# A transformer block with linear attention and routed experts: query chunks started inside the key stage, a reordered passage into the feed-forward stage, and GpSimd's bias sums gathered at the end of the key stage

## What is computed

```python
def attention(x, w_qkv, proj, w_out, b_out):          # x: (4, 1024, 128), 16 heads of 8
    q, k, v = split(x @ w_qkv)
    qp = elu1(einsum('bhnd,hdf->bhnf', q, proj))      # 32 features a head
    kp = elu1(einsum('bhnd,hdf->bhnf', k, proj))      # elu1(a) = a + 1 if a > 0 else exp(a)
    kv = einsum('bhnf,bhnd->bhfd', kp, v)
    den = einsum('bhnf,bhf->bhn', qp, kp.sum(2)) + 1e-8
    return (einsum('bhnf,bhfd->bhnd', qp, kv) / den) @ w_out + b_out

def ffn(x, wr, br, w1, b1, w2, b2):                   # 8 experts, 128 -> 512 -> 128
    e = argmax(x @ wr + br)
    return gelu(x @ w1[e] + b1[e]) @ w2[e] + b2[e]

x = layernorm(x + attention(x, ...))
out = layernorm(x + ffn(x, ...))
```

## Time and profile before

| What | Value |
|---|---|
| Time, median of 3 runs (lowest to highest) | 234.96 us (234.77 to 235.1) |
| The profiled execution's own time | 234.93 us |
| Its span, first to last instruction | 233.2 us |
| PE busy | 202.8 us (87%), 1727 matmuls |
| DVE busy | 154.7 us (66%) |
| ACT busy | 140.2 us (60%) |
| POOL busy | 133.4 us (57%) |
| Mean granted TensorE clock | 0.962 of full |
| Bytes moved | 40.45 MB, 173 GB/s on the mean |
| Chain that ended last, by engine | PE 55%, issue 13%, POOL 12%, DVE 8% |

### The profile page before, as it was taken

One profiled execution on the slowest core, in us unless ns is written; L12 is line 12 of the kernel. 1 busy time (PEld: TensorE's weight loads), 2 busy tenths in 40 slices (PEclk: granted clock), 3 DMA queues, 4 the chain that ended last, 5 costly groups with the idle time before them and its releaser, 6 DMA issues.

```text
span 233.2 us, 5949 instructions
## 1 busy us (share of the span) xinstructions
PE 202.8 (87%) x1727; PEld 159.0 (68%) x1734; DVE 154.7 (66%) x530; ACT 140.2 (60%) x366; POOL 133.4 (57%) x171
## 2 busy tenths in 40 slices
PE   7989999999799998898888389899899999999700
PEld 2668888888555554545442279798799999999600
DVE  1577686877476999889989233247557677777720
ACT  3488887878477576866564045455466667666400
POOL 8329284646500104776768617655776588888770
PEclk9999999999999999999999679999999999999955
DMA  4899999999760000111011467650477678874100
GB/s 119 217 379 409 414 408 410 411 414 375 220 178 0 0 6 12 35 35 47 27 35 46 147 175 217 195 138 20 154 221 220 201 229 236 233 182 133 35 6 0
DMA packets 28416, 40.45 MB, mean 173 GB/s; under 512 B 3497, under 2 KB 18126, under 8 KB 28384
## 3 DMA queue, kind: packets, MB, share of 16 engines
q1 hardware_dynamic: 26112, 35.80, 47.5%
q0 software_dynamic: 2272, 4.27, 5.3%
HBM read 17.95 MB, written 22.56 MB: 174 GB/s over the span
## 4 chain that ended last, share of the span: by engine, by line
PE 55%; issue 13%; POOL 12%; DVE 8%; DMA 4%; ACT 4%; SPq 1%; POOLq 1%; DVEq 0%; ACTq 0%
PE pair L753 15%; PE pair L299 12%; PE pair L768 10%; POOL sorted_rows L504 9%; PE bank L615 4%; PE bank L768 4%; PE pair L746 2%; DMA x_all<-sorted_rows 1%; DVE qexp L969 1%; PE pair L585 1%; POOL rstd L476 1%; ACT qexp L829 1%; DMA w_slot<-in_L_ffn_w_dram 1%; PE bank L595 1%; PE pair L765 1%
## 5 line engine op out<-in xcount | busy, mean ns | idle before, releaser
L912 ACT ACTIVATE qfeat<-pair,w_sb 128x128 f32<-128x128 f32 x156 | 44.7, 368 | 29.1 <-PE pair L753 28.5
L753 PE MATMUL pair<-xsT,w_slot 128*128 128x128 f32 x312 | 42.4, 280 | 1.7 <-DMA w_slot<-in_L_ffn_w_dram 1.2
L504 POOL DMA_INDIRECT sorted_rows<-x,dest x32 | 33.4, 1043 | 17.1 <-DVE dest L1115 9.9
L753 PEld LDWEIGHTS pair<-xsT,w_slot 128*128 128x128 f32 x312 | 38.7, 195 | 2.4 <-issue 2.4
L299 PE MATMUL pair<-wkv_part,xT_all 128*128 128x256 f32 x192 | 33.8, 320 | 2.0 <-ACT vals L839 0.8
L299 PEld LDWEIGHTS pair<-wkv_part,xT_all 128*128 128x128 f32 x192 | 28.3, 188 | 5.5 <-issue 5.5
L768 PE MATMUL pair<-w_sb,qfeat 128*128 x232 | 31.5, 279 | 0.0
L534 POOL TENSOR_TENSOR ksum<-kfeat 128x512 f32<-128x512 f32 x12 | 16.5, 1372 | 24.9 <-DVE kfeat L978 24.9
L525 POOL DMA_INDIRECT out_dram<-x_all x26 | 26.3, 1010 | 7.0 <-issue 5.7
L768 PEld LDWEIGHTS pair<-w_sb,qfeat 128*128 128x128 f32 x232 | 28.2, 192 | 0.9
L476 POOL TENSOR_TENSOR rstd<-var_eps,minus_half 128x4 f32<-128x4 f32 x8 | 8.3, 1041 | 31.4 <-DVE var_eps L1051 31.4
(11 more groups left out here) (181 smaller groups left out, 405.8 us busy)
## 6 DMA issues: line engine op xcount, KB each, us to landing
sorted_rows<-pad_rows SPq DMA_DIRECT2D x11, 1584.0 KB, 22.9
w_slot<-in_L_ffn_w_dram SPq DMA_DIRECT2D x39, 256.0 KB, 3.1
x_all<-in_L_attn_x_dram SPq DMA_DIRECT2D x8, 256.0 KB, 5.4
w_sb<-in_L_ffn_w_dram SPq DMA_DIRECT2D x4, 512.0 KB, 14.0
x_all<-sorted_rows SPq DMA_DIRECT2D x26, 66.0 KB, 2.6
xs<-sorted_rows SPq DMA_DIRECT2D x13, 66.0 KB, 2.3
w_sb<-in_L_ffn_b_dram SPq DMA_DIRECT2D x1, 512.0 KB, 7.2
sorted_rows<-x,dest POOLq DMA_INDIRECT x32, 2.5
```

Of the source, the lines that this page charges most:

```text
L504: g_.indirect_dma_start(out=sorted_rows, out_offset=bass.IndirectOffsetOnAxis(ap=dest[:, ring, i:i + 1], axis=0), in_=x1[:, ring, i, :], i ...
L753: last = mm(h_bank[t % 2][:, k * P:(k + 1) * P], w1_slot[:, t % WB, k * P:(k + 1) * P], xsT[:, t % 2, :], start=True, stop=True)
L912: a_.activation(hT[:, t % 2, k * P:(k + 1) * P], h_bank[t % 2][:, k * P:(k + 1) * P], ACT.Gelu, bias=w2_sb[:, bass.ds(w_at[t] + (FF + D + ...
```

## The change

**Key stage.** GpSimd keeps only the router score (`score_base`) in the loop; the eight sums of x and output bias run one after the other when the loop is over. Three of the four query chunks of group 0 move into the last steps on PE, with their exponentials on ACT and two of DVE's `q_features` ahead of `keep_kv(3)`; the banks of the chunks are rotated by one for that.

**Query stage.** DVE's group step has the same instructions in another order. ACT takes the third exponential ahead of the layer norm.

**Passage.** Both layer norms of GpSimd go to ACT: group 6's at once, group 7's a quarter at a time after the first four tile steps. On PE `project(7)` and `ranks(6)` go ahead of `turn(0)`, with four more unread matmuls between them, and `ranks(7)` comes two tile steps earlier. DVE makes the experts' part of the first table earlier (8 steps, `TAB_E`), and SP asks for the weights of tiles 0 to 3 then; from there on it asks for the weights two tiles ahead of the rows. DVE adds the bias of every tile, so the twenty one-row matmuls in the profile (two for each of tiles 0 to 9) go. The first four batches are normalised one step later.

```diff
-        TAB_A, TAB_B = 14, 16
+        TAB_E, TAB_A, TAB_B = 8, 14, 16
...
-        def offset(eng, kind, table, t, most):
+        def offset(eng, kind, table, t, most, first=TAB_A):
             if t == 0:
-                eng.wait_ge(tab_step, TAB_A)
+                eng.wait_ge(tab_step, first)
...
-        q_bank = [bank[0], bank[1], bank[2], bank[7]]
+        q_bank = [bank[7], bank[0], bank[1], bank[2]]
...
+            def load_weights(t):
                 reach(sp, hid_pre, t - WB + 1)
-                at = offset(sp, ENG.SP, e_tab, t, (E - 1) * FF)
+                at = offset(sp, ENG.SP, e_tab, t, (E - 1) * FF, TAB_E)
                 sp.dma_start(w1_slot[:, t % WB, :], w1_pieces[bass.ds(at, FF), :].rearrange("(p c) d -> p (c d)", c=FC)
                              ).then_inc(w1_loaded[t % WB], 16)
+            for t in range(4):
+                load_weights(t)
             for i in range(XR):
                 sp.wait_ge(scattered[i], 16 * GT * len(range(i, GA, XR)))
             for t in range(NA):
                 load_rows(t)
-
+                if 4 <= t + 2 < NA:
+                    load_weights(t + 2)
+
+            for t in (NA, NA + 1):
+                load_weights(t)
             for i in range(XR):
                 sp.wait_ge(scattered[i], 16 * GT * G // XR)
             sp.wait_ge(res_ready, G)
             for t in range(NA, NT):
                 load_rows(t)
+                if t + 2 < NT:
+                    load_weights(t + 2)
             sp.wait_ge(stored, 16 * NT)
...
+            def score_base(g):
+                tiles = slice(g * GT, (g + 1) * GT)
...
-            def layer_norm(g):
-                par, ring = g % 2, g % XR
-                pool.wait_ge(shift_ready, g + 1)
-                pool.wait_ge(rstd_ready, g + 1)
-                for i in range(GT):
-                    last = g_.tensor_scalar(x1[:, ring, i, 0:D], res[:, par, i, :], rstd[:, par, i:i + 1], shift[:, par, i:i + 1],
-                                            ALU.mult, ALU.add)
-                last.then_inc(x1_ready, 1)
...
-                    residual_base(u // 2)
+                    score_base(u // 2)
+            pool.wait_ge(const_in, 16 * 2)
+            for g in range(G):
+                residual_base(g)
             for s in range(G):
                 group_step(s)
             scatter(G - 4, range(GT))
             token_numbers(G - 2)
             inverse_deviation(G - 2)
-            layer_norm(G - 2)
             scatter(G - 3, range(0, 2))
             token_numbers(G - 1)
             inverse_deviation(G - 1)
             scatter(G - 3, range(2, GT))
-            layer_norm(G - 1)
             scatter(G - 2, range(GT))
...
+            def q_chunk(g, k):
+                n = g * C + k
+                reach(pe, q_done, n - QB + 1)
+                if n in (1, 2):
+                    pe.wait_ge(k_done, T - 1)
+                    pe.wait_ge(v_ready, T - 1)
+                mm(q_bank[n % QB][:, :], ones_bf[:, :], share[:, :].to_broadcast([P, 512]), start=True, stop=False)
+                product(q_bank[n % QB], wq_part[:, :, k * P:(k + 1) * P], xT_all[:, :, g * 512:(g + 1) * 512],
+                        [(slice(0, 512), slice(0, 512))], start=False).then_inc(q_pre, 1)
+
             turn_group(0)
...
             for u in range(UT + 3):
+                if u == UT + 2:
+                    q_chunk(0, 2)
...
                 if 0 <= u - 1 < UT:
+                    if u == UT:
+                        q_chunk(0, 0)
                     add_kv(2 * u - 2)
                     if (u - 1) % UB:
                         add_pair_sum(u - 2)
+                    if u == UT:
+                        q_chunk(0, 1)
                     add_kv(2 * u - 1)
...
-                if t not in BIASED_BY_DVE:
-                    mm(y_bank[t % 4][:, 0:D], ones_row[:, :], w2_sb[0:1, bass.ds(w_at[t] + FF, D)], start=True, stop=False)
                 for k in range(FC):
                     pe.wait_ge(hT_ready, FC * t + k + 1)
                     last = mm(y_bank[t % 4][:, 0:D], hT[:, t % 2, k * P:(k + 1) * P],
-                              w2_sb[:, bass.ds(w_at[t] + k * D, D)], start=(k == 0 and t in BIASED_BY_DVE), stop=(k == FC - 1))
+                              w2_sb[:, bass.ds(w_at[t] + k * D, D)], start=(k == 0), stop=(k == FC - 1))
...
-            pe.wait_ge(q_done, C * (G - 1) + 1)
+            pe.wait_ge(q_done, C * (G - 1) + 2)
             stay_awake(12, bank[0])
             project(G - 2)
             attend(G - 1)
             ranks(G - 3)
             stay_awake(12, bank[2])
+            project(G - 1)
+            stay_awake(4, bank[2])
+            ranks(G - 2)
             turn(0)
             weights_of(0)
             up(0)
-            project(G - 1)
             turn(1)
             weights_of(1)
             tile_step(0)
-            ranks(G - 2)
             tile_step(1)
+            ranks(G - 1)
             tile_step(2)
             tile_step(3)
-            ranks(G - 1)
             for s in range(4, NT):
...
+            def exp_q(g, k):
+                n = g * C + k
+                act.wait_ge(q_pre, n + 1)
+                reach(act, q_done, n - QB + 1)
+                if n in (0, 2, 3):
+                    act.wait_ge(k_done, (T - 2, 0, T - 1, T)[n])
+                a_.activation(qexp[:, (n + 2) % QB, :], q_bank[n % QB][:, :], ACT.Exp, bias=minus_one[:, :]).then_inc(q_exp, 1)
...
             for u in range(UT + 2):
+                if u == UT + 1:
+                    exp_q(0, 0)
+                    exp_q(0, 1)
...
+            def norm_tile(g, i):
                 par = g % 2
                 act.wait_ge(shift_ready, g + 1)
                 act.wait_ge(number_ready, g + 1)
+                last = a_.activation(x1[:, g % XR, i, 0:D], res[:, par, i, :], ACT.Identity,
+                                     bias=shift[:, par, i:i + 1], scale=rstd[:, par, i:i + 1])
+                if i == GT - 1:
+                    last.then_inc(x1_ready, 1)
+
+            def layer_norm(g):
                 for i in range(GT):
-                    last = a_.activation(x1[:, g % XR, i, 0:D], res[:, par, i, :], ACT.Identity,
-                                         bias=shift[:, par, i:i + 1], scale=rstd[:, par, i:i + 1])
-                last.then_inc(x1_ready, 1)
+                    norm_tile(g, i)
...
             def group_step(s):
-                if s < G:
+                if 0 < s < G:
                     exp_q(s, 0)
                     exp_q(s, 1)
+                if s < G:
+                    exp_q(s, 2)
                 if 0 <= s - 3 < G:
                     layer_norm(s - 3)
-                if s < G:
...
             a_.preload_act_table_set("gelu_and_others")
+            layer_norm(G - 2)
             keep_rows(0)
             gelu(0)
             keep_rows(1)
-            for s in range(NT):
+            for s in range(GT):
+                tile_step(s)
+                norm_tile(G - 1, s)
+            for s in range(GT, NT):
                 tile_step(s)
...
+            q_features(0, 0)
+            q_features(0, 1)
+            keep_kv(B - 1)
...
                 attn, route, row = 0 <= s - 2 < G, 0 <= s - 3 < G, 0 <= s - 4 < G
                 if attn:
                     newton_first(s - 2)
-                if route:
-                    shift_of(s - 3)
                 if row:
                     row_numbers(s - 4)
                 if attn:
                     newton_second(s - 2)
-                if route:
-                    scale_scores(s - 3)
                 if row:
                     next_rows(s - 4)
                     pick_rows(s - 4)
                 if attn:
                     normalise(s - 2)
+                if route:
+                    shift_of(s - 3)
+                if row:
+                    rows(s - 4)
...
                 if route:
+                    scale_scores(s - 3)
+                if s:
+                    q_features(s, 0)
...
                     add_row(s)
-                    if s in BIASED_BY_DVE:
-                        add_bias(s)
+                    add_bias(s)
                     row_statistics(s)
...
             rows(4)
             used_rows(region)
+            q_features(7, 3)
+            used_tiles()
+            shift_of(5)
+            tiles_as_floats()
+            scale_scores(5)
+            tab().tensor_tensor_scan(tiles_end[:, 1:E + 1], ones_e[:, :], tiles_f[:, :], 0.0, ALU.mult, ALU.add).then_inc(tab_step, 1)
...
+            first_weights_of(first)
+            assert done[0] == TAB_E
             choose(5)
...
             rows(5)
             shift_of(6)
+            weights_of(0)
             scale_scores(6)
+            add_x(7)
             bias_scores(6)
+            add_x_score(7)
             best_score(6)
+            statistics(7, 0)
...
+
+            add_row(0)
+            shift_of(7)
+            add_bias(0)
+            scale_scores(7)
+            row_statistics(0)
```

(1 more changed line is left out.)

157 lines of the change are left out of this document (59 added, 98 removed).

## The result

The changed kernel takes 223.5 us (median of four runs, 222.57 to 225.5) where the kernel before takes 234.87 beside it: ratio 0.953, 95% interval 0.946 to 0.959. On a second chip it was 223.5 again (six runs, 222.21 to 225.52), ratio 0.945 (0.939 to 0.952). The forecast was 220.0, with 218.0 to 224.8 for the range: the sign and the range held, and 3.5 of the 14.9 us did not come. The profiled execution of the first comparison took 223.68, its span is 222.0. The ratios leave disturbed runs out (those over 1.5% above the same kernel's fastest), the medians count every run, and the profiled runs of two experiments, the earlier choice and the bias by PE, are disturbed ones.

The account below looks back on a forecast made before the run. PE, busy 87% of the span, bounds the kernel, with DVE setting the query stage's pace. Terms 0.5 + 1.8 + 2.4 + 4.7 + 5.5 = 14.9 off 234.93 give 220.0 us, range 218.0 to 224.8.

Parts of the forecast that it names:

- GpSimd's sums: Key stage: eight sums move to GpSimd's idle time, so DVE's minimum is no longer held; gain 0.5 us, bounds 0 to 1.0.
- Query chunks: End of key stage: three query chunks of group 0 fill PE's idle time; gain 1.8 us, bounds 1.35 to 2.79.
- Order in the group step: Query stage: DVE's shift goes behind attnT, its 0.57 wait for GpSimd's power goes; period 7.29, gain 2.4 us, bounds 0 to 3.0.
- the two rules: Second Newton step beside GpSimd's power: the trace says not slowed (220.0 us), the Trainium skill says blocked (222.4).
- The rival with chance 0.08: Query stage: the Newton step waits for GpSimd's power instead of the shift, keeping 0.57 a group; 222.4 us, chance 0.08.
- Passage: Query stage to tile 6: earlier project(7) and ranks(6), no slow clock; turn of tile 6 at +25.85, gain 4.7 us, bounds 2.0 to 6.0.
- and without the slow clock: Passage: up(0) starts at +13.9 instead of +14.4, with PE's clock not fallen to its lower level.
- the rival with chance 0.18: Passage: the clock falls all the same, matmuls of two tiles take about double; 2.5 us more, 222.5, chance 0.18.
- Bias by DVE: Feed-forward stage: DVE adds the bias, six tile steps of 2.58 become 1.90; gain 5.5 us, bounds 3.5 to 6.0.
- Tile 13: Feed-forward stage: its rows land by +37, its turn at +39.4, margin 2 us; a rival had them late, 222 to 225, chance 0.09.
- the main forecast: Whole kernel: all terms near their values, 220.0 us, from 218 to 222, chance 0.61.
- the rivals: Whole kernel: clock, Newton step and late tile 13, together chance 0.35, to 225 us; slower 0.02; no change 0.02.

Follow-up runs that it names:

- awake_b: Changed kernel with 18 more unread matmuls on PE in the passage's gaps: 221.73 us, beside 223.5 for the changed kernel.
- both_b: Changed kernel with 18 more unread PE matmuls in the passage and DVE's choice of group 7 ahead of the first residual sums: 219.7 us, ratio to before 0.930.
- insums: Changed kernel with GpSimd's sums of x and bias back in the key stage's loop: 248.51 us on the slower chip; as insums_b on a third chip 223.16.
- early: Changed kernel with DVE's choice of group 7 ahead of the first residual sums: 246.95 us on the slower chip; beside the changed kernel (223.5) on another chip 220.94.
- the last four: Changed kernel with one term undone each, on a third chip: query chunks 224.56 us, shift order 226.16, bias of tiles 0 to 9 233.71, GpSimd's sums 223.16.

## Why the prediction was right, and where it was off

- **GpSimd's sums**, 0.5 forecast: 0.4 measured in the key stage (54.19 against 53.8), nothing in the median time. The mechanism is the forecast one, a held minimum and PE's wait behind it.
- **Query chunks**, 1.8 forecast: 1.5 measured in the same way (55.29 against 53.8), 1.1 in the median time. Before, the stretch from the minimum at 16.95 to group 0's first Newton step took 55.92 (72.87), so the two terms together brought 2.1. Of it 0.3 is not accounted for by either undone edit alone; undoing both together was not tried.
- **Order in the group step**, 2.4 forecast: 2.7 measured. DVE does set the pace, the period became 7.22 (forecast 7.29), and PE's waits for `attnT` there went, all but 0.25 before the passage's own.
- **Where the two rules differed**: the power did not hold the Newton step (0.69 beside it). The rival with chance 0.08 did not come.
- **Passage**, 4.7 forecast: 0.85 in the profiled run. This is the term that was mis-sized. `up(0)` started at +14.44 (forecast +13.9), still at full clock; `up(1)` started at +17.91 (+16.95) and ran at half speed; the turn of tile 3 came at +21.46 (+18.85). The step that failed is "and without the slow clock": closing the gap of 3.77 left several of 0.4 to 1.6 with little between them, and the fall came as before, only after `up(0)`. This was the rival with chance 0.18 and a price of 2.5 (222.5). It measured 2.7 in the passage of the first profile and 4.1 in that of the second; the filled gaps gave 1.8 in the median time. The other 1.2 of the first profile is seen in `awake_b`, whose clock stays full. There the turn of tile 3 comes at +19.30 instead of +18.85, so 0.45 is in the handovers before it. The wait for the choice of group 7 cost 1.9, with what hangs on it, where I had 1.3 (1.1 and 0.2 for ACT's norms). The full clock alone does not give the forecast time: `awake_b` is at 221.7. `both_b`, at 219.7, has the earlier choice too, which was not in the sum, so it does not confirm 220.0.
- **Bias by DVE**, 5.5 forecast: 5.13 from tile 6 to 13 (18.40 to 13.27) and 0.4 for the restart behind them. The 2.58 a step that I read was a mean: one step of 2.93 and five of 2.50. The undone edit gives 6.5, which includes the tiles of the passage, where I had put nothing.
- **Tile 13** was in time, as forecast, and even in `both_b`, which turns it at 152.26. But the margin was not the forecast 2. The rows were asked for 3.76 before the turn, and 3.48 before it in `both_b` (at 148.78), where a fetch took 3.16: 0.6 and 0.3 are left. GpSimd's last scatter ended at +36.3, not +32. (My turn at +39.4 should have been +39.15.) The tiles behind it were less safe than I took them to be: tile 14 waits in `awake_b`, tiles 15, 16 and 21 are late in `both_b`, tile 16 in the changed kernel on the second chip, each time for 0.5 to 1.2 us with the restart.

The sum in the two profiled traces, stretch by stretch: to group 0's first Newton step 2.07 (72.87 to 70.80), from there to group 6's 2.59 (45.37 to 42.78), the passage 0.85, tiles 6 to 13 5.13, tile 13 to 14 0.42, from tile 14 to the end 0.14. Together 11.2, the difference of the spans (233.2 to 222.0). Of the 14.9 forecast 3.85 are missing in the passage; every other stretch is within 0.25 of its term. The time came out beyond the 218 to 222 of the main forecast, which had 0.61; the stated range held because it left room for the rivals.

A better version came out of it: `both_b`, 18 unread matmuls more and group 7's choice ahead of the first residual sums, 219.7 us against 223.5 beside it, 0.983 of the changed kernel's median. On the slower chip the same kernel was no better than `insums` (248.53 against 248.51), and `early` alone was faster (246.95).

## What to carry to other kernels

When one long gap is cut into several short ones with thin work between them, don't count on the clock: price the stretch at both levels and give the low one the larger chance. It fell in every profile of the changed passage but those of `awake_b` and `both_b`, whose gaps are filled, and on the slower chip, with longer waits, it fell in spite of the filling. Unread matmuls in the gaps bought 1.8 us here; moving the choice behind them forward bought about as much again, and the two gains nearly added. Put the version that you compare with into every group of runs: four runs on a slower chip told almost nothing without it, and the last four lack it too. And to measure a term of a few tenths, count from an instruction near it in the same trace, not from the start of the span or by the time of the whole kernel: that is how the sums' 0.4 was found.

## What was unexpected in the hardware

- Two runs of the same program had the clock fall at 129.4 and at 127.6 us, and passages of 29.7 and 31.1 us, though their first Newton steps of group 6 were 0.1 us apart (113.58 and 113.69).
- The clock fell with no gap on PE above 1.6 us in the passage, and stayed low for 10.2 us on the second chip, though PE was busy for 7.97 of the 10 us from 128 to 138 (its windows, above).
- Another chip ran the kernel before in 255.84 us against 234.9. Up to group 3 its trace is the same within 0.1 us (group 3's first Newton step at 92.20 in `insums`, 92.26 in `insums_b`); behind it DVE waits 0.7 to 2.6 for ACT at single groups, and tile steps reach 4.3 us instead of 1.9. What makes it slower stays open.
